# A Mamba-2 layer with a routed FFN on one Trainium2 core: the decay matrix by Exp from broadcast rows and a GpSimd select, in place of two matmuls and one Exp

## The reference, cut to what matters

```python
dt = softplus(dt + dt_bias);  A_dt = dt * -exp(A_log)
A_cs = cumsum(A_dt)                              # in a chunk, per head
Lmat = exp(where(tril, A_cs[l] - A_cs[s], -inf)) # token l, earlier token s
Y_diag = einsum('bcln,bcsn,bhcls,bcshp->bclhp', Cc, Bc, Lmat, Xc)
states = einsum('bcln,bhcl,bclhp->bchpn', Bc, exp(A_cs[-1] - A_cs), Xc)
...                                              # states carried from chunk to chunk
Y_off  = einsum('bcln,bchpn,bhcl->bclhp', Cc, states_prev, exp(A_cs))
```

## Time and profile before

| | |
|---|---|
| median of 3 runs | 794.13 us (787.53 to 796.54) |
| the profiled execution | 795.79 us, its span 794.0 us |
| busy share of the span | PE 79%, PEld 67%, DVE 74%, ACT 58%, POOL 50% |
| 300 to 400 us | PE 94.06 us, PEld 78.67, DVE 86.41, ACT 78.41, POOL 68.00 |
| 520 to 780 us (experts) | PE 205.72 us of 260, DVE 144.40, ACT 121.66, POOL 133.79 |
| granted clock | 0.938 over the span |

### The profile page before, as it was taken

How to read it: one execution, slowest core, us unless ns; L and a number is a source line. 1 busy time by engine, 2 the same in 40 slices (tenths; PEclk the granted TensorE clock), 3 DMA queues, 4 the chain that set the end, 5 groups by cost and what they waited for, 6 DMA issues and landing times. The chain is left out here.

```text
span 794.0 us, 15139 instructions
## 1 busy us (share of the span) xinstructions
PE 631.2 (79%) x3701; PEld 531.9 (67%) x3703; DVE 585.2 (74%) x1410; ACT 462.3 (58%) x1014; POOL 400.4 (50%) x601
## 2 busy tenths in 40 slices
PE   0695629998999989999998998699898889988700
PEld 0695317777778777778777776587777777777600
DVE  7787898898898888888898888555565555654445
ACT  0352446688777878877788775454555555554400
POOL 3000006576766766766676767145555555555510
PEclk9999999799999999999999999799999999999955
DMA  9950100000000000000000015133333333333169
GB/s 306 266 130 0 29 1 23 19 27 23 29 22 22 28 22 22 28 22 22 25 26 22 29 24 184 36 88 99 97 85 96 88 98 98 85 98 86 54 252 382
DMA packets 64647, 61.43 MB, mean 77 GB/s; under 512 B 9242, under 2 KB 55710, under 8 KB 64624
## 3 DMA queue, kind: packets, MB, share of 16 engines
q1 hardware_dynamic: 56176, 44.11, 19.7%
q0 software_dynamic: 8448, 17.06, 6.2%
HBM read 30.19 MB, written 31.47 MB: 78 GB/s over the span
## 5 line engine op out<-in xcount | busy, mean ns | idle before, releaser
L449 POOL DMA_INDIRECT moe_d<-raw,slot_st x136 | 133.8, 984 | 124.6 <-issue 102.1
L422 POOL DMA_INDIRECT slots_d<-rows,slot_st x128 | 134.6, 1052 | 73.8 <-POOL rows L417 52.5
L1040 DVE SCALAR_TENSOR_TENSOR act<-raw,taps,act 128x512 f32<-128x512 f32 x192 | 149.3, 785 | 23.9 <-ACT act L513 23.1
L398 POOL TENSOR_TENSOR xde<-xb,e_end 128x256 f32<-128x256 f32 x64 | 45.6, 713 | 113.2 <-DVE xb L1117 111.6
L1233 DVE CAST x_hi<-bank 128x256 fp32r<-128x256 f32 x68 | 28.8, 424 | 95.4 <-PE bank L871 91.8
L864 PE MATMUL bank<-xw_hi,x_hi 128*128 x136 | 61.1, 449 | 27.2 <-DVE x_lo L1235 22.7
L774 PE MATMUL bank<-xb,m_sb 128*128 128x64 f32 x512 | 75.9, 298 | 3.8 <-POOL xde L398 3.8
L774 PEld LDWEIGHTS bank<-xb,m_sb 128*128 128x128 f32 x512 | 73.1, 216 | 5.6 <-issue 3.9
L890 PE MATMUL bank<-act,raw 128*128 x544 | 72.0, 275 | 1.8 <-issue 1.8
L664 ACT ACTIVATE raw<-bank 128x256 f32<-128x256 f32 x68 | 26.5, 391 | 77.2 <-remote 68.5
L890 PEld LDWEIGHTS bank<-act,raw 128*128 128x128 f32 x544 | 66.1, 192 | 1.9 <-issue 1.9
(11 more groups left out here) (231 smaller groups left out, 1659.4 us busy)
## 6 DMA issues: line engine op xcount, KB each, us to landing
slots_d<-rows SPq DMA_DIRECT2D x8, 1122.0 KB, 13.4
rows<-slots_d SPq DMA_DIRECT2D x68, 132.0 KB
x_sb<-in_x SPq DMA_DIRECT2D x8, 512.0 KB, 7.0
act<-in_x SPq DMA_DIRECT2D x64, 64.0 KB
xw_hi<-moe_d SPq DMA_DIRECT2D x8, 512.0 KB, 9.3
xw_lo<-moe_d SPq DMA_DIRECT2D x8, 512.0 KB, 9.9
out<-x_sb SPq DMA_DIRECT2D x8, 512.0 KB, 13.5
moe_d<-raw,slot_st POOLq DMA_INDIRECT x136
```

Of the source, the lines that this page charges most:

```text
L398: nc.gpsimd.tensor_tensor(by_head(xde[:, u, :]), by_head(xdt[:, u, :]), per_head(e_end, nn), ALU.mult).then_inc(xde_done, 1)
L422: nc.gpsimd.indirect_dma_start(out=slots_d, out_offset=bass.IndirectOffsetOnAxis(ap=slot_st[:, r, c:c + 1], axis=0), in_=rows[:, r, c, :], ...
L449: nc.gpsimd.indirect_dma_start(out=moe_d, out_offset=bass.IndirectOffsetOnAxis(ap=slot_st[:, r, c:c + 1], axis=0), in_=ym[r][:, c * D:(c + ...
L1040: V.scalar_tensor_tensor(out=group_act(par)[:, t, :], in0=proj[:, t, k:k + GT], scalar=taps[:, t, k:k + 1], in1=group_act(par)[:, t, :], o ...
```

## The change: what it does

- `exponents` is gone from PE, with `dd_l`, `dd_r`, `mask_b`, `ident_b` and their setup.
- The transposed cumulative sums are copied once in full precision (`cs_t`) and stored with one transfer. SP loads, for two tiles, the 1024 values of the sums as one row, sent to all 128 partitions (`cs_row`, 4 KB per partition, 512 KB, two places).
- ACT computes exp(cs[l] - cs[s]) head by head: input the row, bias the column of `ncs` (the negated sums, by token on the partitions). It gives `l_exp`.
- POOL sets the part below the diagonal to zero in place, over all four heads at once (`causal`), and gives `l_done`, which DVE waits for. It stands between the row copy and the two scatters of the tile before.

```diff
-            def dd_loads(b):
+            def row_loads(b):
                 for i in range(SC // 2):
-                    if not (is_first(b) and i < 2):
-                        sp.wait_ge(dd_done, b * SC + 2 * i - 2)
-                    n = b * SC + 2 * i
-                    sp.dma_start(dd_l[0:8, i % 2, :, :].bitcast(F32), ncs_d[:, bass.ds(n, 2), :])\
-                        .then_inc(ld_dd[i % 2], 16)
-                    sp.dma_start(dd_r[8:10, i % 2, :].bitcast(F32), cs_d[:, bass.ds(n * NH * P, 2 * NH * P)])\
-                        .then_inc(ld_dd[i % 2], 16)
+                    n = b * SC + 2 * i
+                    if not (is_first(b) and i < 2):
+                        sp.wait_ge(l_exp, n - 2)
+                    sp.dma_start(cs_row[:, i % 2, :], cs_d[:, bass.ds(n * NH * P, 2 * NH * P)]
+                                 .broadcast_to([P, 2 * NH * P])).then_inc(ld_cs[i % 2], 16)
...
+            def causal(nn, u):
+                pool.wait_ge(l_exp, nn + 1)
+                pool.sem_inc(scatters, 1)
+                lh = l_sb[:, u, :].rearrange("p (h l) -> p h l", h=NH)
+                nc.gpsimd.affine_select(out=lh, in_=lh, compare_op=ALU.is_ge, fill=0.0, base=0,
+                                        pattern=[[0, NH], [1, P]], channel_multiplier=-1).then_inc(l_done, 1)
...
                     prepare_rows(b, j)
+                    if not (is_last(b) and j == SC - 1):
+                        causal(nn + 1, (j + 1) % 2)
                     scatter(j % R, 0)
                     scatter(j % R, 1)
...
-            def decays(nn, u):
-                act_e.wait_ge(dd_done, nn + 1)
-                A(l_sb[:, u, :], bank[2][:, :], ACT.Exp).then_inc(l_done, 1)
+            def decays(b, j):
+                nn, u, pr, o = b * SC + j, j % 2, (j // 2) % 2, (j % 2) * NH * P
+                act_e.wait_ge(ld_cs[pr], 16 * (b * 2 + j // 4 + 1))
+                if not (is_first(b) and j < 2):
+                    act_e.wait_ge(m_done, nn - 1)
+                for h in range(NH):
+                    a = A(l_sb[:, u, h * P:(h + 1) * P], cs_row[:, pr, o + h * P:o + (h + 1) * P], ACT.Exp,
+                          bias=ncs[:, tile_ix(nn), h:h + 1].rearrange("p a h -> p (a h)"))
+                a.then_inc(l_exp, 1)
...
-            def exponents(b, j):
-                nn, pr, o = b * SC + j, (j // 2) % 2, j % 2
-                pe.wait_ge(ld_dd[pr], 32 * (b * 2 + j // 4 + 1))
-                if not (is_first(b) and j < 1):
-                    pe.wait_ge(l_done, nn)
-                mm(bank[2][:, :], dd_l[:, pr, o, :], dd_r[:, pr, o * NH * P:(o + 1) * NH * P], start=True, stop=False)
-                mm(bank[2][:, :], ident_b[:, :], mask_b[:, :].unsqueeze(1).broadcast_to([P, NH, P]),
-                   start=False, stop=True).then_inc(dd_done, 1)
...
-            V.tensor_copy(hi, tp).then_inc(csp_done, 1)
...
-            V.tensor_scalar(nhi, hi.bitcast(F32), -1.0, None, ALU.mult).then_inc(csp_done, 1)
-            V.tensor_scalar(nlo, lo.bitcast(F32), -1.0, None, ALU.mult).then_inc(csp_done, 1)
+            V.tensor_copy(cs_t[:, :, :], bank[6][:, 0:2 * P].rearrange("p (k l) -> p k l", k=2)).then_inc(cst_done, 1)
+            V.tensor_scalar(ncs[:, :, :], cs_sb[:, :, :], -1.0, None, ALU.mult).then_inc(ncs_done, 1)
```

More of the change, by code:

```diff
@@ L75, in program @@
         moe_d = nc.dram_tensor("moe_d", (K * NT * P, D), F32, kind="Internal").ap()
-        cs_d = nc.dram_tensor("cs_d", (2, NT * NH * P), F32, kind="Internal").ap()
-        ncs_d = nc.dram_tensor("ncs_d", (2 * NH, NT, P), F32, kind="Internal").ap()
+        cs_d = nc.dram_tensor("cs_d", (1, NT * NH * P), F32, kind="Internal").ap()
         x_sb = sb("x_sb", [P, NT, D])
@@ L176, in program @@
         ld_x = [sem(f"ld_x{i}") for i in range(8)]
-        ld_dd = [sem(f"ld_dd{i}") for i in range(2)]
+        ld_cs = [sem(f"ld_cs{i}") for i in range(2)]
         scat = [sem(f"scat{i}") for i in range(R)]
@@ L365, in _ @@
             pool.tensor_copy(rows[:, 0, 0, D:D + 1], tokid[:, 0:1]).then_inc(consts, 1)
-            for t, v in ((ident, 0.0), (upper, 1.0), (strict_b, 1.0), (mask_b, 0.0)):
+            for t, v in ((ident, 0.0), (upper, 1.0), (strict_b, 1.0)):
                 chain(pool.memset(t[:, :], v))
@@ L376, in _ @@
                                      pattern=[[1, P]], channel_multiplier=-1))
-            chain(pool.affine_select(out=mask_b[:, :], in_=mask_b[:, :], compare_op=ALU.is_ge, fill=MASKED, base=0,
-                                     pattern=[[1, P]], channel_multiplier=-1))
-            ind = ddr0[0:8, :].rearrange("p (h l) -> p h l", h=NH)
-            chain(pool.memset(ddr0[0:8, :], 0.0))
-            for part in range(2):
-                chain(pool.affine_select(out=ind, in_=ind, compare_op=ALU.not_equal, fill=1.0, base=NH * part,
-                                         pattern=[[1, NH], [0, P]], channel_multiplier=-1))
             chain(pool.iota(rev_i, pattern=[[-1, E]], base=E, channel_multiplier=0))
@@ L387, in _ @@
             pool.wait_ge(consts, 1)
-            chain(pool.iota(tokid, pattern=[[1, NT]], base=0, channel_multiplier=NT))
-            pool.tensor_copy(ident_b[:, :], ident[:, :]).then_inc(consts, 1)
+            pool.iota(tokid, pattern=[[1, NT]], base=0, channel_multiplier=NT).then_inc(consts, 1)
             pool.wait_ge(norm_done, 2)
@@ L591, in sequence @@
                     if q < 3:
-                        decays(nn + 1, (j + 1) % 2)
+                        decays(b, j + 1)
                     for c in {2: (j, j + 1), 3: ()}.get(q, (j,)):
@@ L621, in sequence @@
                             act_e.wait_ge(m_done, nn + 1)
-                            decays(nn + 2, j % 2)
+                            decays(b, j + 2)
                         if not (first and j < 4):
@@ L828, in sequence @@
                         front(b, j + 1)
-                    if q == 2 and not (last and g == 1):
-                        exponents(b, j + 2)
                     if q == 2 and not last:
@@ L961, in _ @@
             dve.wait_ge(w_hi_done, 3)
-            chain(V.tensor_tensor(w_lo[:, :], w_ln, w_hi[:, :].bitcast(F32), ALU.subtract))
+            V.tensor_tensor(w_lo[:, :], w_ln, w_hi[:, :].bitcast(F32), ALU.subtract).then_inc(wdve_done, 1)
             dve.wait_ge(consts, 2)
-            for i in range(2):
-                for a in range(2):
-                    last = V.tensor_copy(dd_r[0:8, i, a * NH * P:(a + 1) * NH * P], ddr0[0:8, :])
-            last.then_inc(wdve_done, 1)
             V.tensor_copy(rev, rev_i)
```

46 lines of the change are left out of this document (15 added, 31 removed).

## The result

The changed kernel takes 818.0 us (median of four runs; the kernel before beside it 793.9): ratio 1.032, interval 1.029 to 1.036. Direction and range held, the size did not: I forecast +10.9 us, measured are +24.1. The profiled execution took 818.1 us; its span is 816.4, before it was 794.0.

A forecast was written before the change was run, and what follows sets the result against it. Bound: PE early in a group (slow groups), then a chain ACT, DVE, ACT. 795.8 + 10.6 (loop) + 1.5 (last tiles) - 1.0 (setup) = 806.9, less 1.7 for the median: 805 us, range 782 to 822.

The forecast's parts named there:

- the select's term: POOL, between row copy and scatters: select 0.72 us, queue grows 0.5, round 5.4 inside a 5.93 tile, covered in the loop.
- Rival 4: POOL becomes the bound: long gap stays, select at upper bound, round 6.2 us against 5.93, +17 us, 812; chance 0.13.
- The Exps' size: ACT: four 128x128 Exps for one 128x512, +0.68 us queue per tile, +1.16 per fast group.
- the set ahead of the second tile's row: ACT before L506: 0.20 us of slack there, so the tap and DVE's dense stretch slip by 0.48 us.
- The set after Silu: ACT behind Silu: puts L506 a little behind its matmuls, but PE wants that copy only later; hidden.
- The set before the table load: ACT directly before the Silu table load: +0.68 us per group, nothing covers it.
- PE's relief: PE: 64 exponent matmul pairs go, 0.65 us each; counts after Silu in slow groups, -0.65 us, nothing in fast groups.
- Rival 3: Clock: second half-clock stretch per group, in the third tile, 823 us; sign: clock row below 0.90; chance 0.10.
- Rivals 1 and 2: 1: cheap ACT sets, PE's relief comes through, 783 us, chance 0.20. 2: slack swallows both, 794 us, chance 0.15.
- the 0.53 of rival 1: Group 0.53 us shorter if each ACT set costs the lower bound of 0.16 us queue per Exp, 8 us in all.
- Start: Setup before the loop: four DVE casts and two cumulative-sum operations go, first select +0.35; together -1.0 us.
- The last tiles' cost: Last four tiles, no projections, PE already waits for xde: three selects cost all they take, +1.5 us.

The follow-up runs named there:

- the select alone: Kernel before with only POOL's select added between row copy and scatters, exponent matmuls and one Exp kept: 821.6 us, 1.030; with filler of two and three matmuls 1.011.
- the filled kernel before: Kernel before plus two and three unread matmuls in PE's two waits around Silu: 784.1 us, 0.986; on another chip 754.5 us, 0.986.
- the filled kernel with the Exps: Changed kernel without the select, plus seven and three unread matmuls on PE around Silu: 771.9 us, 1.010.
- each half alone: Kernel before with only the select added on POOL: 821.6 us, 1.030; kernel before with only the Exp split in four from PSUM: 820.3 us, 1.028.
- both attempts here: Select alone, filled, on a scratch buffer, m waiting only for Exps: 1.019, 1.017 with smaller filler; filled changed kernel, select ahead of row copies: 1.039.

## Why the prediction was right or wrong

- **The step that failed is the select's term.** The prediction said "so it is covered there": POOL's round was priced at 5.4 us inside a tile of 5.93 and the loop's charge set to zero; and of DVE the prediction said that no operand of the loop changes. Measured with filler the select costs 0.95 to 1.06 us per group, 12 to 14 us over 13 groups; the whole error of the forecast is 13.2 us. It is paid on DVE, whose m waits (0.60 us per group, by the select alone) and whose taps and gates grow (0.52 and 0.15), and DVE's second half of a group is on the path, as the prediction itself had found. Rival 4 drew on the Trainium skill (GPSIMD Engine Reference, Specifications), by which GpSimd contends for SBUF with VectorE's instructions that have two SBUF inputs, and noted that "the taps' own loss is not in this price"; that loss was about half of the cost. The trace agrees with the rule: a gate that starts behind a select takes 0.85 us for 0.41, and m, with one input in PSUM, keeps its 0.68. POOL itself did not become the bound: with the full change it still waits for ACT's rows, 20.9 us in the 290 from 190 to 480.
- **The Exps' size held, their places did not.** +1.16 us per fast group was forecast, +1.33 measured (typical groups, 24.20 on 22.87). But the set ahead of the second tile's row, priced at 0.48, is hidden: the L506 ahead of it waited 1.09 us for PE in the filled kernel before and for nothing in the filled kernel with the Exps, so that the L506 behind the set comes no later in the group, 12.30 us behind the table load for 12.46. The set after Silu, called hidden, costs 0.70, because the first tap, and with it DVE, comes later by the whole set. Two errors that cancel, so the size was right by luck. The set before the table load costs 0.67 as forecast 0.68.
- **PE's relief**: the forecast gave 0.65 us in slow groups alone, 0.45 on average, and nothing in fast ones. At full clock nothing showed, as said: groups of 24.0 with the matmuls and 24.2 without them. What the clock costs fell by 0.54 us per group from the kernel before to the changed one (0.92 to 0.38). That lies near the 0.45, but the two are not shown to be the same thing: giving PE the work back in the changed kernel cost 0.09, and taking it away where there is no select was worth 0.94. So the relief's worth hangs on what stands beside it, and the agreement has luck in it.
- **The sum again**: -0.54 by the clock, +1.40 Exps, +0.95 select: +1.81 per group, as measured. It has to come out, since each term is the difference of two neighbouring kernels; what it tells is the size of each term beside the forecast's -0.45, +1.16 and 0. The select's is the one that is off.
- **Rival 3** (clock): its signs in the trace came, the clock row at 0.88 and half-clock stretches that begin in the third tile, and it was still wrong. With the clock back at 0.97 the loop is 0.38 us per group shorter, of 1.81. The prediction's test for it was bad: a low clock is a cost only where PE is what the group waits for.
- **Rivals 1 and 2** are out; the Exp's price of 397 ns alone excludes the first. Two rivals' prices do not fit the prediction's own sum: rival 4's 812 is 17 on the 795 of the kernel before and leaves out the +10.9 of the rest (with it 822), and the 0.53 of rival 1 counts 0.04 us of unused slack as a gain. Start (-1.3 for -1.0) and loads (no wait) held. The last tiles' cost came, 3.5 for 1.5, but not by the step given: PE's waits for `xde` did not grow (0.73 and 2.00 us for 0.83 and 2.33), and without the select these tiles take 34.0 us, 2.8 of the 3.5 more than before. The clock in them was 0.73 for 0.94. With filler the select is worth 2.6 us there (35.5 for 32.9), with the clock at 0.82 and 0.87; how the 3.5 divide is open:

```profile
509.58 1.07 PE L760 MATMUL bank<-xb,m_sb 128*128 128x64 f32 x8 [0.73 <-POOL xde L376]
...
515.13 1.85 PE L760 MATMUL bank<-xb,m_sb 128*128 128x64 f32 x8 [2.00 <-POOL xde L376]
```

What stays open: of the 1.06 us of the select alone some 0.65 hang on its size and 0.41 on its being there at all. The traces show both ways by which it acts, DVE's instructions that start behind a select and those that meet POOL's moved `xde`, `state_k` and row copy; the share of each in the group was not measured. That would take work on POOL of the same length that leaves SBUF alone.

## What to carry to other kernels

Work put on GpSimd beside a dense VectorE is not covered by GpSimd's free time: charge VectorE's instructions that it and the GpSimd work behind it meet, here about a quarter of a microsecond per 0.7 us select. Taking VectorE's wait for it away is no cure by itself: both attempts here made the groups longer (24.5 for 23.9, 25.5 for 25.2). Before parts of a change are priced one by one, hold TensorE's clock: here each half alone measured nearly as dear as the whole, and only with filler in TensorE's waits did the parts add up. A few matmuls that nobody reads, put into a wait that leads into TensorE's own bottleneck, were worth 1.4% by themselves; in the changed kernel, where TensorE was no longer the bottleneck, they were worth 0.4 us of a 25.5 us group and nothing in the whole time.

## What the runs showed of the hardware that I had not expected

- The level of the clock follows PE's pauses by this much: with waits of 2.28 and 0.92 us around Silu the granted clock was 0.50 for about 10 us, and the group 3.5 us longer (27.4 for 23.9); with five matmuls in those waits it was 0.97 over the loop, and 1.00 in the kernel before.
- The kernel before takes 795 to 797 us on three of the chips and 766 on two. The filled kernel before ran on one of each kind, and at the start of the experts' stage they are alike to 0.1 us (its table load at 492.31 and 492.22). The spans are 782.1 and 752.4: all 30 us lie in the experts. There the first chip has PE less busy, the other more (the same stretch of each):

```profile
540.00:640.00 100.00, 88.15 (x569) 76.54 (x569) 57.32 (x173) 52.70 (x142) 56.10 (x57) 1.00 0.33 92
```

```profile
540.00:640.00 100.00, 95.34 (x642) 85.05 (x642) 62.78 (x193) 61.87 (x161) 62.91 (x65) 1.00 0.37 105
```

and the first one alone has a wait of ACT that the profile can't put to an engine (us in total, times, longest, over 540 to 735 us):

```profile
ACT raw L664 <- remote: 62.8, 25, 2.7
```

What that is was not tried.
- A select on GpSimd took 0.64 us in half of the tiles of the changed kernel and up to 1.20 us beside DVE's work; the first scatter followed it after 0.16 us, and ahead of the select stand 0.33 us after the row copy. The 0.82 us gap between copy and scatter of the earlier trace rows was gone, so the queue grew by about 0.4 us (0.76 + 0.33 + 0.16 - 0.82; 0.5 priced).
